# Offset convolution in four 32-column groups, the later images' first statistics beside attention 0, and the constants made behind the first norm

## The chip, the cores and the metric

The kernel runs on one core of a Trainium2 chip. The metric is the device time of one execution in microseconds (us), the median of several runs. In this text PE is TensorE (PEld its weight loads), ACT is ScalarE, DVE is VectorE, POOL is GpSimd and SP is SyncE, which here only issues transfers.

## The reference, cut to what matters

Four images x of 128 channels and 64 x 64 pixels pass four layers. Each layer starts with a group norm over 32 groups of four channels (no learned scale) and adds its result to x.

```python
x = x + layer0(_gn(x))   # attention of 4096 x 4096 scores per image, keys used as values too
x = x + layer1(_gn(x))   # involution: per-pixel 3 x 3 weights made by two 1 x 1 convolutions
x = x + layer2(_gn(x))   # 7 x 7 depthwise convolution, layer norm, MLP with gelu
x = x + layer3(_gn(x))   # deformable 3 x 3 convolution, batch norm, relu
# inside layer 3:
om = conv3x3(x, offset_w) + offset_b          # 128 -> 27 channels: 18 offsets, 9 masks
```

The change touches the 3 x 3 convolution that makes `om`, the first group norm of an image, and the preparation of constants before the first image.

## The kernel before

All engines run one hand-written program each; semaphores with counts (`wait_ge`, `then_inc`) order them. An image's 4096 pixels are handled as `NCH` = 8 chunks of 512 columns or `T` = 32 tiles of 128. There are eight PSUM banks, named in pairs `O`, `ST`, `MX`, `TR`.

**Start.** SP loads image 0 into `x_cur` and then 23 weight tensors (`w_in`). POOL clears and builds `ident`, `fold`, `gavg` and others (`pool_setup`). PE, DVE, ACT and POOL then wait for all weights and make derived constants: a bf16 high and low part of the involution weights `l1w2_s` (for this ACT first copies a bias row with three small transfers, `b2_in`, L746), the offset weights `offwb`, batch norm factors and more. Only when that is done (`dve_setup`) does each engine enter `sample(0, False)`.

**One image, `sample(n, dcn)`.** DVE waits for `x_in`, takes `bn_stats` of the eight chunks of `x_cur` (L1052) and runs `group_norm` with PE and POOL: mean over the group by a matmul with `gavg`, deviation, a second matmul, a power on POOL, the factors in `gst`. ACT then writes the normed image `xn` in four quarters (L756). From the second image on, DVE next runs `indices(n - 1)` (L1303 on), the bilinear addresses and weights for the last layer of the image before. Then comes `attention(n, dcn)`: keys and values chunk by chunk, row maxima of the first chunk (`first_maxima`, L422, reduced on DVE at L1097), and 256 steps. A step is four bf16 matmuls for scores (L464 to L467), one exponent on ACT (L779), four f32 matmuls with the values (L477) and one bf16 matmul for a maximum (L432), reduced on DVE (L1102). In images 1 to 3 the deformable convolution of the image before is run between these steps: POOL gathers patches (L1465), ACT and DVE weigh them, PE convolves. For the last image it is a tail of its own.

**End of an image, `layer3_prepare(n)`.** After the fourth norm ACT writes `xn` and its bf16 high part `xh` quarter by quarter, and DVE the low part `xl` (`low_part`, L1077, eight quarters per image over two layers). PE works on pairs of chunks: for both chunks 18 matmuls of 128 weight columns each (L668, L670). The weights hold the 27 high columns, the 27 low columns and zeros; they meet `xh` and `xl`, so rows 0 to 26 and 27 to 53 of a bank hold partial sums. Then for each chunk come four transposes of the image (L678, for the patch table) and four matmuls with `fold` (L684), which transpose and add the partial sums. ACT copies the image chunk to `xst` (L932) and evacuates the bank with the bias (L935); DVE evacuates the transposes (L1294) and the offsets (L1296). When all offsets are there (`om_rdy`), `indices` can start. SP writes the patch table in two halves of eight transfers (L352), each half as soon as the transposes of four chunks are evacuated. POOL starts gathering when `idx_rdy` and all 16 transfers of the table (`tbl_w`) are there, and in images 1 to 3 after its key work. SP loads the next image into `x_cur` when the last quarter of `xh` is written (L356).

```python
with pe.Fori(0, NCH // 2 - 1) as j:
    wait_alone(pe, s["xl_rdy"], 8 * n + 6 + j)
    two_chunks(j)
two_chunks(NCH // 2 - 1)
```

Of the kernel before, what the change touches and what calls it, by code (L numbers as in the profile page):

```python
# [13 lines left out]
BF16 = mybir.dt.bfloat16  # L14
# [49 lines left out]
def build(nc, x, wq, wk, l1w1, l1w2, l1gb, l2w1, l2w2, offw, offb, dcnw, vecs, out):  # L64
    ctx = ExitStack()
    with ctx:
# [20 lines left out]
        offwb = sb("offwb", [C, K1, 128], BF16)  # L87
# [48 lines left out]
        gst = sb("gst", [128, 8])  # L136
        ist = sb("ist", [128, NCH, 6])
# [9 lines left out]
        w2st = regk[:, 0:K1 * C].rearrange("p (k c) -> p k c", c=C)  # L147
        w2rest = regk[:, K1 * C:2 * K1 * C].rearrange("p (k c) -> p k c", c=C)
# [12 lines left out]
        slots = G[:].rearrange("p a k n -> p (a k) n")  # L161
        prod = [G[:, 0], G[:, 1], valt]
# [68 lines left out]

        def not_first(n):
            return not (isinstance(n, int) and n == 0)
# [4 lines left out]
        def wait_alone(eng, semaphore, value):  # L238
# [9 lines left out]
            "w_in pool_setup dve_setup pe_setup b2_rows b2_in bn_ve bn_pow zeroed "  # L248
# [20 lines left out]
        def _(sp):  # L269
# [39 lines left out]
            def sample(n, dcn, more):  # L309
# [4 lines left out]
                for i in range(NCH):  # L314
# [56 lines left out]
        def _(pe):  # L371
# [4 lines left out]
            pe.wait_ge(s["w_in"], 16 * WEIGHTS)  # L376
            pe.wait_ge(s["pool_setup"], 1)
            for f in range(FT):
                last = mm(P[0][:, f:f + 1], l2w1_s[:, f * 128:(f + 1) * 128], vec[:, LNB:LNB + 1],
                          start=True, stop=True)  # L380
            last.then_inc(s["pe_setup"], 1)
            nc.tensor.transpose(P[1][0:K1, 0:C], vec[:, L1B:L1B + K1], ident[:]).then_inc(s["pe_setup"], 1)
            pe.wait_ge(s["dve_setup"], 1)

            def group_norm(gi):
                pe.wait_ge(s["gn_stats"], gi + 1)
                mm(O[0][:, 0:1], gavg[:], gst[:, 0:1], start=True, stop=True).then_inc(s["gn_grp"], 1)
                pe.wait_ge(s["gn_dev"], gi + 1)
                mm(O[1][:, 0:1], gavg[:], gst[:, 3:4], start=True, stop=True).then_inc(s["gn_grp"], 1)

            def q_project(n, i):

                if i == 1:
# [5 lines left out]
            def key_chunk(n, c):  # L399
                wait_alone(pe, s["gn_xn"], 16 * n + c // 2 + 1)  # L400
                if c >= 2:
# [12 lines left out]
            def first_maxima(n, mc):  # L414

                pe.wait_ge(s["kh_rdy"], NCH * n + mc + 1)
                pe.wait_ge(s["q_rdy"], NCH * n + 1)
                for t in range(TB):
# [86 lines left out]
            def attention(n, dcn):  # L505
# [20 lines left out]
                for at in range(STEPS):  # L526
# [133 lines left out]
            def layer3_prepare(n):  # L660

                def two_chunks(j):
                    for u in range(2):
                        c = j * 2 + u
                        pe.wait_ge(s["oc_ev"], NCH * n + c + 1)
                        for k in range(K1):
                            dy, dx = k // 3 - 1, k % 3 - 1
                            mm(as_rows(ST[u][:]), offwb[:, k, :], shifted(c, dy, dx, xh),  # L668
                               start=(k == 0), stop=False)
                            last = mm(as_rows(ST[u][:]), offwb[:, k, :], shifted(c, dy, dx, xl),  # L670
                                      start=False, stop=(k == K1 - 1))
                        last.then_inc(s["oc_ps"], 1)
                    for u in range(2):
                        c = j * 2 + u
                        pe.wait_ge(s["xs_rdy"], NCH * n + c + 1)
                        pe.wait_ge(s["xt_ev"], NCH * n + c + 1)
# [859 lines left out]
```

## Time and profile before

| what | value |
|---|---|
| time, three runs | 4579.86, 4582.22 (median), 4582.42 us |
| time of the profiled execution | 4579.79 us |
| its span, first to last instruction | 4577.9 us |
| PE busy | 3952.1 us, 86% |
| DVE busy | 2862.4 us, 63% |
| ACT busy | 1779.5 us, 39% |
| POOL busy | 1454.8 us, 32% |
| mean granted clock of PE | 0.912 of full speed |

Busy time is the union of an engine's instructions. A matmul's shown duration holds its way through the pipeline, so back-to-back matmuls overlap in the record, and the distance from start to start is their price. The granted clock is given as a share of 2.4 GHz; 0.50 is 1.2 GHz.

### The profile page before, as it was taken

To read this page: it belongs to the slowest core of one execution; us is meant where nothing else is said; L and a number is where in the kernel's file an instruction comes from. 1 tells how busy PE (TensorE), PEld (TensorE's weight loads), DVE (VectorE), ACT (ScalarE), POOL (GpSimd) and SP (SyncE) were. 2 spreads that over 40 slices of the span, in tenths; PEclk is the share of its full clock that TensorE was granted. 3 is DMA by queue.
4 is the path that set the end of the run, shared out by engine and by line. 5 is a ranking of instruction groups with operands and counts; after the bars stand their busy time and mean duration, and the time that the engine had idled before them with its cause. 6 is when DMAs were issued, how large, how long until landed. Compare 5 with 4: busy or idle time off the path is not lost.

```text
span 4577.9 us, 63042 instructions
## 1 busy us (share of the span) xinstructions
PE 3952.1 (86%) x22185; PEld 2641.7 (58%) x22185; DVE 2862.4 (63%) x6449; ACT 1779.5 (39%) x3733; POOL 1454.8 (32%) x1433
## 2 busy tenths in 40 slices
PE   5999978979999968978999977988999996985555
PEld 3777733437777843435778753434787772433444
DVE  4333257757777637847777737847777746863665
ACT  2333342234555532234555543223555544122333
POOL 2000040026444323006444404005444414003775
PEclk9999989989999989988999988988999997996555
DMA  1000000045444300035445410016454420005775
GB/s 44 10 8 10 24 5 1 0 131 170 146 146 144 108 24 1 0 110 153 144 144 151 136 30 1 0 47 176 143 152 134 148 68 0 1 18 161 216 218 177
DMA packets 206392, 400.54 MB, mean 87 GB/s; under 512 B 23090, under 2 KB 121805, under 8 KB 204585
## 3 DMA queue, kind: packets, MB, share of 16 engines
q0 software_dynamic: 92160, 302.06, 22.8%
q1 hardware_dynamic: 113906, 94.92, 7.0%
q8 instruction: 162, 2.65, 0.2%
q14 instruction: 110, 0.89, 0.1%
q10 hardware_dynamic: 54, 0.01, 0.0%
HBM read 337.36 MB, written 59.53 MB: 87 GB/s over the span
## 4 chain that ended last, share of the span: by engine, by line
PE 73%; POOL 9%; issue 6%; DVE 5%; POOLq 3%; ACT 2%; DVEq 1%; DMA 1%; SPq 0%; ACTq 0%
PE bank L477 20%; PE bank L605 11%; PE bank L464 5%; PE bank L465 5%; PE bank L466 5%; PE bank L467 5%; PE bank L500 4%; PE bank L432 4%; POOL G L1465 3%; PE bank L491 2%; PE bank L631 2%; POOLq L1438 2%; PE bank L647 2%; PE bank L668 1%; PE bank L670 1%
## 5 line engine op out<-in xcount | busy, mean ns | idle before, releaser
L477 PEld LDWEIGHTS bank<-vt,pt 128*128 128x128 f32 x8192 | 1073.6, 192 | 145.6 <-issue 0.2
L477 PE MATMUL bank<-vt,pt 128*128 128x129 f32 x8192 | 1078.4, 275 | 0.0
L1102 DVE TENSOR_REDUCE mxc<-bank 128x1 f32<-128x512 f32 x896 | 617.9, 691 | 696.6 <-PE bank L432 693.8
L779 ACT ACTIVATE pt<-bank 128x512 f32<-128x512 f32 x1024 | 611.4, 597 | 905.9 <-PE bank L467 904.4
L1465 POOL DMA_INDIRECT G<-patch_table,idx x576 | 557.3, 967 | 479.9 <-DVEq L1141 248.1
L1245 DVE SCALAR_TENSOR_TENSOR G<-xn,vec,G 128x512 f32<-128x512 f32 x736 | 521.7, 748 | 47.2 <-issue 40.7
L464 PE MATMUL bank<-qh,regk 128*128 128x512 bf16 x1024 | 390.1, 381 | 3.1 <-ACT m L765 3.1
L465 PE MATMUL bank<-ql,regk 128*128 128x512 bf16 x1024 | 390.1, 381 | 0.0
L466 PE MATMUL bank<-qh,regk 128*128 128x512 bf16 x1024 | 390.1, 381 | 0.0
L467 PE MATMUL bank<-m,ones 128*128 128x512 bf16 x1024 | 389.9, 381 | 0.0
L605 PE MATMUL bank<-vt,val 128*128 (+1 forms) x1152 | 372.6, 389 | 19.5 <-DVE xl L1077 19.5
L1138 DVE SCALAR_TENSOR_TENSOR val<-G,w,val 128x128 f32<-128x128 f32 x1296 | 375.3, 346 | 7.9 <-issue 0.4
L1417 POOL TENSOR_TENSOR gst<-gst,mhalf 128x1 f32<-128x1 f32 x16 | 8.9, 558 | 1108.0 <-DVE gst L1067 1108.0
L432 PE MATMUL bank<-regk,qh 128*128 128x512 bf16 x896 | 341.8, 383 | 5.2 <-DVE mxc L1097 2.7
L1465 POOL DMA_INDIRECT regq<-patch_table,idx x256 | 245.4, 959 | 261.8 <-DVEq L1141 190.2
L1465 POOL DMA_INDIRECT x_cur<-patch_table,idx x256 | 246.9, 964 | 192.0 <-DVEq L1141 120.4
L1448 POOL TENSOR_TENSOR rs<-ve,mhalf 128x4 f32<-128x4 f32 x32 | 36.2, 1131 | 819.1 <-ACT ve L899 819.1
L500 PE MATMUL bank<-valt,dcnw_s 128*128 128x128 f32 x1728 | 240.3, 275 | 0.0
L500 PEld LDWEIGHTS bank<-valt,dcnw_s 128*128 128x128 f32 x1728 | 233.7, 191 | 11.3 <-issue 1.5
L802 ACT ACTIVATE valt<-bank 128x384 f32<-128x384 f32 x288 | 141.0, 490 | 213.9 <-PE bank L491 213.9
L605 PE MATMUL bank<-xl,val 128*128 (+1 forms) x576 | 224.0, 389 | 0.0
L605 PEld LDWEIGHTS bank<-vt,val 128*128 128x128 bf16 x1152 | 113.6, 99 | 180.0 <-issue 37.5
(231 smaller groups left out, 5913.7 us busy)
## 6 DMA issues: line engine op xcount, KB each, us to landing
patch_table<-valt SPq DMA_DIRECT2D x64, 512.0 KB, 7.1
G<-patch_table,idx POOLq DMA_INDIRECT x576, 3.7
x_cur<-in_x SPq DMA_DIRECT2D x4, 2048.0 KB, 7.9
xl<-in_x SPq DMA_DIRECT2D x32, 256.0 KB, 3.3
attn_out<-ob SPq DMA_DIRECT2D x32, 256.0 KB, 2.3
x_store<-x_cur SPq DMA_DIRECT2D x4, 2048.0 KB, 6.3
xr<-x_store SPq DMA_DIRECT2D x32, 256.0 KB, 5.4
out<-fo SPq DMA_DIRECT2D x32, 256.0 KB, 3.5
```

What stands on the lines that cost most here:

```text
L432: mm(MX[at % 2], qh[:, q0:q0 + 128], kh[:, mc * CH:(mc + 1) * CH], start=True, stop=True)\
L464: mm(bank, kh[:, tile], cols(qh, i % Q_RING), start=True, stop=False)
L465: mm(bank, kh[:, tile], cols(ql, i % Q_RING), start=False, stop=False)
L466: mm(bank, kl[:, tile], cols(qh, i % Q_RING), start=False, stop=False)
L467: mm(bank, ones2[:], m2[:, i % 2, :], start=False, stop=True).then_inc(s["st_rdy"], 1)
L477: last = mm(O[t // 2][:, (t % 2) * (C + 1):(t % 2 + 1) * (C + 1)], pt[:, at % PT_RING, t * 128:(t + 1) * 128], vt[:, st, :], start=(st == ...
L500: last = mm(TR[0][:, 384:512], dcnw_s[:, k, :], valt[:, k, piece], start=(k == 0), stop=(k == K1 - 1))
L605: last = mm(as_rows(ST[u][:]), diag(k, part), shifted(c, k // 7 - 3, k % 7 - 3, image), start=(k == 0 and image is xh and part == 0), stop ...
L779: A(pt[:, at % PT_RING, :], ST[at % ST_RING], ACT.Exp, scale=SCALE).then_inc(s["exp_done"], 1)
L1102: v.reduce_max(mxc[:, t, mc:mc + 1], MX[at % 2], AX.X).then_inc(s["mx_red"], 1)
L1245: v.scalar_tensor_tensor(acc, src, wgt, acc, ALU.mult, ALU.add)
L1465: g.indirect_dma_start(out=patches(j, k), out_offset=None, in_=table[:], in_offset=bass.IndirectOffsetOnAxis(ap=idx[:, j * K1 + k:j * K1 + ...
```

## The change

1. **Offset convolution.** `offwb` holds for each tap a 32-column block with the high part and one with the low part (27 columns used). A chunk gets 27 matmuls (per tap high x `xh`, high x `xl`, low x `xh`; low x `xl` is no longer computed). Each has 32 weight columns and writes one of four groups of 32 PSUM partitions in turn. `fold` adds four groups instead of two. PE goes chunk by chunk: the 27 matmuls of chunk c, the transposes of chunk c, the fold matmuls of chunk c - 1. Each chunk waits only for its own quarter of `xl`. The program is written out instead of looping. DVE's third and fourth quarter of `xl` come behind the first two image evacuations, and ACT copies an image chunk one ahead.
2. **Statistics.** SP loads images 1 and 2 into the idle `G` buffer behind the first table clears, and image 3 into the same place once image 1 was read. In attention 0 DVE takes their chunk statistics at every second step from steps 40, 90 and 140 on, and PE, DVE and POOL run the group norm arithmetic for each between the steps, into `gx`. Images 1 to 3 start with ACT's norm straight from `gx`; DVE goes from `layer3_prepare` directly to `indices`.
3. **Start.** The first image's statistics and norm come before the derived constants. DVE's `setup()` follows the norm; ACT's three bias row transfers follow its four norm activations. PE's first `first_maxima` and ACT's second `q_evacuate` wait for `dve_setup`. The staging area `w2st` moves from `regk` to `valt`.
4. Semaphore indices of the norms are renumbered (`norm_index`), and a few waits that the loops or the setup gave for free are written out.

```diff
-        offwb = sb("offwb", [C, K1, 128], BF16)
+        offwb = sb("offwb", [C, K1, 2, 32], BF16)
+        gx = sb("gx", [128, N, 8])
+        x_ahead = [G[:].rearrange("p a k n -> p (a k n)")[:, b * L:(b + 1) * L] for b in range(2)]
+        def ahead(q):
+            return 40 + 50 * (q - 1)
+        def image_quarter(c):
+            return min(3, (ROWS * c + ROWS) // (H // 4))
...
+            for q in range(1, 3):
+                sp.dma_start(x_ahead[(q - 1) % 2], x[q]).then_inc(s["xg_in"], 16)
...
+                    if not dcn and i == 1:
+                        sp.wait_ge(s["gn_stats"], norm_index(1, 0) + 1)
+                        sp.dma_start(x_ahead[0], x[3]).then_inc(s["xg_in"], 16)
...
+                    if not dcn:
+                        for q in range(1, N):
+                            if at == ahead(q) + 20:
+                                group_norm_first(norm_index(q, 0), TR[0], gx[:, q, :])
+                            if at == ahead(q) + 23:
+                                group_norm_second(norm_index(q, 0), TR[0], gx[:, q, :])
...
+                def offsets(c):
+                    pe.wait_ge(s["xl_rdy"], 8 * n + 4 + image_quarter(c) + 1)
+                    pe.wait_ge(s["oc_ev"], NCH * n + c + 1)
+                    for at in range(3 * K1):
+                        k, (part, image) = at // 3, ((0, xh), (0, xl), (1, xh))[at % 3]
+                        col = 32 * (at % 4)
+                        last = mm(as_rows(ST[c % 2][col:col + 32, :]), offwb[:, k, part, :],
+                                  shifted(c, k // 3 - 1, k % 3 - 1, image),
+                                  start=(at < 4), stop=(at >= 3 * K1 - 4), skip_group_check=True)
+                    last.then_inc(s["oc_ps"], 1)
...
+                for c in range(NCH):
+                    offsets(c)
+                    image_rows(c)
+                    if c:
+                        offset_rows(c - 1)
+                offset_rows(NCH - 1)
...
+            def bias_rows():
+                act.wait_ge(s["b2_rows"], 1)
+                for row in range(96, 99):
+                    act.dma_start(w2st[row:row + 1], ob[0:K1, 0:C]).then_inc(s["b2_in"], 16)
+                act.wait_ge(s["w_in"], 16 * WEIGHTS)
...
+                image_copy(0)
+                for c in range(NCH):
+                    if c + 1 < NCH:
+                        image_copy(c + 1)
+                    offset_evacuate(c)
...
+            def norm_ahead(q, r):
+                if r % 2 == 0 and 0 <= r < 2 * NCH:
+                    if r == 0:
+                        dve.wait_ge(s["xg_in"], 16 * q if q < 3 else 48)
+                    chunk_stats(r // 2, x_ahead[(q - 1) % 2])
+                if r == 18:
+                    norm_collect(gx[:, q, :])
+                if r == 21:
+                    norm_mean(norm_index(q, 0), gx[:, q, :], TR[0])
+                if r == 24:
+                    norm_variance(norm_index(q, 0), gx[:, q, :], TR[0])
+                if r == 26:
+                    norm_finish(norm_index(q, 0), gx[:, q, :])
...
+                low_part(2 * n + 1, (0, 1))
+                for c in range(NCH):
+                    image_evacuate(c)
+                    if c:
+                        offset_evacuate(c - 1)
+                    if c < 2:
+                        low_part(2 * n + 1, (c + 2,))
+                offset_evacuate(NCH - 1)
...
             def sample(n, dcn):
-                wait_alone(dve, s["x_in"], 16 * (n + 1))
-                for c in range(NCH):
-                    chunk_stats(c)
-                group_norm(4 * n)
+                if n == 0:
+                    dve.wait_ge(s["x_in"], 16)
+                    for c in range(NCH):
+                        chunk_stats(c)
+                    group_norm(norm_index(0, 0))
+                    setup()
```

## Rows read from the trace of the kernel before

**Rows 1.** Page, chain of work that ended last, by engine:
```profile
PE 73%; POOL 9%; issue 6%; DVE 5%; POOLq 3%; ACT 2%; DVEq 1%; DMA 1%; SPq 0%; ACTq 0%
```

**Rows 2.** Windows around image 0's last stage; time is busy us (count), then clock, DMA:
```profile
core 0: us, PE busy (x) PEld busy (x) DVE busy (x) ACT busy (x) POOL busy (x), PEclk, DMA share, GB/s
930.60:936.90 6.30, 0.01 (x1) 0.02 (x1) 2.46 (x2) 6.30 (x6) 1.56 (x2) 0.50 0.20 83
936.90:940.70 3.80, 3.80 (x10) 1.42 (x11) 2.11 (x2) 3.41 (x4) 0.00 (x0) 0.51 0.02 4
940.70:980.40 39.70, 39.70 (x232) 23.30 (x230) 7.72 (x16) 10.48 (x16) 0.00 (x0) 1.00 0.55 158
```

**Rows 3.** Timeline of PE, one pair of chunks, image 3: start, duration, instruction:
```profile
4133.69 0.38 PE L668 MATMUL bank<-vt,offwb 128*128 x1
...
4141.55 0.60 PE L678 MATMUL bank<-ident,xst 128*128 128x128 f32 x4
4141.98 0.97 PE L684 MATMUL bank<-fold,val 128*128 128x27 f32 x8
...
4144.08 0.38 PE L668 MATMUL bank<-vt,offwb 128*128 x1
```

**Rows 4.** Timeline, image 0's last stage and what follows it:
```profile
930.58 1.25 ACT L756 ACTIVATE xn<-x_cur,gst 128x1024 f32<-128x1024 f32 x1 [4.94 <-DVE gst L1069]
...
939.69 0.62 ACT L932 ACTIVATE xst<-xn 128x512 f32 x1
939.82 1.23 DVE L1077 TENSOR_TENSOR xl<-xn,vt 128x1024 bf16<-128x1024 f32 x1 [1.04 <-ACT vt L756]
...
980.56 0.27 DVE L1296 COPY regq<-bank 128x108 f32 x1
...
980.97 4.84 DVE L1052 BATCH_NORM_STATS2 bst<-x_cur 128x6 f32<-128x512 f32 x8
...
989.15 0.30 DVE L1307 CAST regq<-regq 128x288 f32<-128x288 int32 x1
```

**Rows 5.** Timeline of PE inside attention 0, four small transposes:
```profile
143.77 0.38 PE L443 MATMUL bank<-identb,mhl 128*2 128x128 bf16 x4
```

**Rows 6.** Timeline of the SP queue and POOL, image 3's table and the first gather:
```profile
4144.37 26.92 SPq L352 DMA_DIRECT2D patch_table<-valt  x12
...
4165.09 14.96 SPq L352 DMA_DIRECT2D patch_table<-valt  x8
...
4185.62 1.06 POOL L1465 DMA_INDIRECT G<-patch_table,idx  x1 [68.87 <-DMA patch_table<-valt]
```

**Rows 7.** Timeline of attention 0, two successive steps, DVE:
```profile
421.23 0.69 DVE L1102 TENSOR_REDUCE mxc<-bank 128x1 f32<-128x512 f32 x1 [1.28 <-PE bank L432]
...
423.20 0.69 DVE L1102 TENSOR_REDUCE mxc<-bank 128x1 f32<-128x512 f32 x1 [1.28 <-PE bank L432]
```

**Rows 8.** Timeline of the kernel's start, all engines:
```profile
13.13 0.52 POOL L1407 TENSOR_SCALAR_AFFINE_SELECT gavg<-gavg 128x128 f32<-128x128 f32 x1
...
22.08 1.87 PE L379 MATMUL bank<-vec,l2w_s 128*128 128x1 f32 x8 [22.08 <-DMA l1gb_s<-in_l1gb]
...
24.61 2.87 ACTq L746 DMA_DIRECT2D regk<-xst  x3
...
29.00 0.76 DVE L1022 CAST l1w_s<-regk 128x1152 bf16<-128x1152 f32 x1 [3.48 <-DMA regk<-xst]
...
36.65 0.21 DVE L1035 TENSOR_TENSOR dwl<-vec,dwh 128x49 f32<-128x49 f32 x1
...
38.76 4.85 DVE L1052 BATCH_NORM_STATS2 bst<-x_cur 128x6 f32<-128x512 f32 x8
...
47.64 1.28 ACT L756 ACT_TABLE_LOAD   x1 [47.64 <-DVE gst L1069]
48.94 4.67 ACT L756 ACTIVATE xn<-x_cur,gst 128x1024 f32<-128x1024 f32 x4
...
57.03 2.48 DVE L1097 TENSOR_REDUCE mxc<-bank 128x1 f32<-128x512 f32 x4 [2.07 <-PE bank L422]
```

**Rows 9.** Transfers of the first 60 us: size in KB, us from issue to landing:
```profile
x_cur<-in_x SPq DMA_DIRECT2D x1, 2048.0 KB, 8.0
```

More of the change, by code:

```diff
@@ L230, in tile_at, with norm_index @@
             return None
+        def ahead(q):
+            return 40 + 50 * (q - 1)
+        def norm_index(n, stage):
+            return N + 3 * n + stage - 1 if stage else n
+        def image_quarter(c):
+            return min(3, (ROWS * c + ROWS) // (H // 4))
         def not_first(n):
@@ L417, in first_maxima @@
                 pe.wait_ge(s["q_rdy"], NCH * n + 1)
+                if mc == 0 and n:
+                    pe.wait_ge(s["ot_ev"], NCH * n + 2)
+                elif mc == 0:
+                    pe.wait_ge(s["dve_setup"], 1)
                 for t in range(TB):
@@ new lines, in image_rows, with offset_rows @@
+                def image_rows(c):
+                    pe.wait_ge(s["xs_rdy"], NCH * n + c + 1)
+                    pe.wait_ge(s["xt_ev"], NCH * n + c + 1)
+                    for t in range(TB):
+                        last = nc.tensor.transpose(TR[c % 2][:, t * 128:(t + 1) * 128],
+                                                   xst[:, c % 2, t * 128:(t + 1) * 128], ident[:])
+                    last.then_inc(s["xt_ps"], 1)
+                def offset_rows(c):
+                    pe.wait_ge(s["oc_ev"], NCH * n + c + 1 + 2)
+                    pe.wait_ge(s["ot_ev"], NCH * n + c + 1)
+                    for t in range(TB):
+                        last = mm(MX[c % 2][:, t * NOFF:(t + 1) * NOFF], om54[:, c % 2, t * 128:(t + 1) * 128],
+                                  fold[:], start=True, stop=True)
+                    last.then_inc(s["ot_ps"], 1)
@@ L741, in _, with group_norm @@
             act.sem_inc(s["oc_ev"], 2)
-            act.wait_ge(s["w_in"], 16 * WEIGHTS)
-            act.wait_ge(s["pool_setup"], 1)
-            act.wait_ge(s["b2_rows"], 1)
-            for row in range(96, 99):
-                act.dma_start(w2st[row:row + 1], xst[0:K1, 0, 0:C]).then_inc(s["b2_in"], 16)
-            act.wait_ge(s["dve_setup"], 1)
-            def group_norm(gi, parts=False):
+            def group_norm(gi, g, parts=False):
                 act.wait_ge(s["gn_ready"], gi + 1)
@@ L828, in attention @@
                 values(NCH - 1)
+                if n == 0:
+                    act.wait_ge(s["dve_setup"], 1)
                 q_evacuate(n, 1)
@@ L1169, in attention @@
                         q_low(n, i + 2)
+                    if not dcn:
+                        for q in range(1, N):
+                            norm_ahead(q, at - ahead(q))
                     if dcn:
@@ L1398, in _ @@
                             pattern=[[-1, 128]], channel_multiplier=1)
-            for half in range(2):
-                g.affine_select(out=fold[:], in_=fold[:], compare_op=ALU.not_equal, fill=1.0, base=-half * NOFF,
+            for quarter in range(4):
+                g.affine_select(out=fold[:], in_=fold[:], compare_op=ALU.not_equal, fill=1.0, base=-quarter * 32,
                                 pattern=[[-1, NOFF]], channel_multiplier=1)
```

256 lines of the change are left out of this document (131 added, 125 removed).

## The prediction

> **What bounds the kernel.** I read the chain that ended last first: 73% of it is PE [rows 1]. So an edit counts where PE, or what PE waits for, gets shorter. The change works at three kinds of place, which I read by windows and then instruction by instruction: the last stage of each image, the seam between two images, and the first 60 us. In the last stage PE is busy without a gap for 39.7 us at the full clock, while DVE has 7.7 and ACT 10.5 us of work [rows 2]: it is bound by PE alone. At the seam the offsets are complete at 980.83, and DVE spends until 989.15 on the next image's statistics and norm before `indices` begins; the attention waits for DVE there. At the start nothing of the image is touched until 38.76 [rows 8].
>
> **Part 1, the offset convolution.** From 4133.69 to 4141.55 PE runs the 36 matmuls of a pair, 0.218 us each. Transposes and folds then take until 4144.08, 2.53 us for two chunks [rows 3]. So a chunk costs 3.93 + 1.27 = 5.2 us now, and the 1.27 stays. The new cost is X for 27 matmuls.
>
> No row of this kernel has matmuls in column groups, so X is bounded.
> - Lowest: four groups stream side by side, each matmul for 0.218 us: 27 / 4 x 0.218 = 1.47 us. Can PE be fed that fast? The four little transposes of [rows 5], each a weight load and a matmul of 128 columns, are recorded as 0.38 us together; one alone lasts 0.218, so they start 0.054 us apart. 27 x 0.054 = 1.46 us: feeding is no tighter than streaming.
> - Middle: the loads pace them. The eight fold matmuls with 128 f32 weight columns take 0.97 us together, of which one's own passage is 0.27 at most, so about 0.1 us each even with few columns [rows 3]. At 0.108, 27 give 2.9 us.
> - Highest: no overlap at all, 27 x 0.218 = 5.9 us, more than the 3.93 of today.
>
> I take 1.47 plus a drained pipeline on entering and leaving the groups. A matmul of 0.38 shown duration and 0.218 spacing leaves 0.16 us, twice, so X = 1.8. It is near the low bound because the nearest row for feeding, [rows 5], shows pairs at 0.054 with narrow weights, and these are narrow too.
>
> The Trainium skill bears on this in two ways. Its page "TensorE: Matmul & The Clock Gate", section "Measured speedup vs the span model", gives 3.07 times for four row tiles and says column tiles come within a few ns; by that X would be near 1.9, an estimate. The section "The mechanism" there says that weight loads overlap matmuls in flight only when the row group differs, which all 27 here share; what that would make of the time is rival C below.
>
> Now the stage, counted from the start of ACT's norm, 930.58 [rows 4]. Today it is 49.8 us to the end of the last fold at about 980.4. After the change:
> - ACT's order is the first limit. Its norm ends at 939.7 where the copy L932 begins, and PE's transposes of chunk 0 need that copy: 9.1 + 0.62 + 0.08 = 9.8. The convolution of chunk 0 comes before, from the first quarter of `xl`, and is hidden.
> - Transposes of chunk 0: 0.45.
> - Seven chunks, each X + 1.27: 7X + 8.9. In today's 39.7 us ACT works 10.48 us and DVE 7.72 for eight chunks [rows 2], 1.3 and 1.0 us a chunk, both below X + 1.27, so PE stays the bound. DVE's third quarter of `xl` now comes after the first image evacuation, near 943, and is needed by chunk 3, after 946.
> - The last fold, 0.82 plus 0.16 of pipeline.
> - Clock: PE stood still before and starts at 0.50 to 0.51; the first ten matmuls today take 3.8 us instead of about 2 [rows 2]. The new order leaves PE idle again after chunk 0, so I charge 2 us.
>
> Together 22.1 + 7X: 34.7 us at X = 1.8, 15.1 us less than 49.8. For images 0 to 2 that is on the path, since `indices` waits for the offsets: 45.3 us.
>
> For image 3 something else is late next, the patch table. Today SP issues the first eight transfers at 4144.37, the second eight from 4165.09 for 15.0 us, and the last lands 5.6 us after that, when POOL starts at 4185.62 [rows 6]. That is 70.4 us after the norm's start at about 4115.2, which stands 49.8 us before the end as in image 0. In the new order four chunks are evacuated at 9.8 + 0.45 + 2 + 3X + 3.0 + 0.9 = 16.1 + 3X (21.5), and eight at 21.2 + 7X (33.8). SP needs 15 us for each half, so it is SP that decides: 21.5 + 15 + 15 + 5.6 = 57.1, 13.3 us less. `indices` is done before that, 15 us after the offsets. In images 0 to 2 the same table lands at 57, while the gathers start near 66 behind POOL's key work. Part 1 gives 45.3 + 13.3 = 58.6 us.
>
> **Part 2, the statistics.** At each of three seams DVE drops the stretch from 980.97 to 989.15, 8.2 us [rows 4]; `indices` follows the offsets directly. ACT's norm needs only `gx`, the image (loaded from about 940 on; such a load took 8.0 us [rows 9]) and the last `xl`, so it starts at the same offset to `indices` as now and the overlap of both stays. 3 x 8.2 = 24.6 us.
>
> The work goes into attention 0. There a step lasts 1.97 us (421.23 to 423.20) and DVE is busy 0.69 of it [rows 7]. A chunk's statistics cost 4.84 / 8 = 0.61 us of spacing, at every second step: 1.3 us of 1.97, and the two maximum banks let PE run on meanwhile. Without this cover 24 x 0.61 = 14.5 us would come back. PE does pay: six one-column matmuls with `gavg`, two f32 passes each at the folds' pace of about 0.11, 1.3 us. The steps between the parts (18, 20, 21, 23, 24, 26) give every answer a step or more; SP's added wait at its second store is for a norm nine steps past, and nothing behind it is urgent. Part 2 gives 23.3 us.
>
> **Part 3, the start.** Everything of [rows 8], in order. The image has landed by about 9 us [rows 9]. POOL's setup ends at 13.65, now 0.4 later for two more selects, and four little DVE operations follow: statistics from 15.0. From 38.76 to 47.64 statistics and norm take 8.9 us: ready at 23.9. ACT loads its table and norms, 1.28 + 4.67: 29.9. Its three transfers (2.87 to issue, the last lands 1.5 later) end at 34.3. SP's two loads of 2 MB for images 1 and 2 start near 31.5 and share the transfer engines with them; I add 2 us: 36.3. Seven to eight wide operations on the weights, 29.00 to 36.65: dve_setup at 44.0. DVE's `q_low` over 512 columns comes next (0.8 us, as the 0.76 of such wide operations), and the first maximum at 44.8 instead of 57.03. The small operations of setup and PE's part (22.08 plus 2.2) are done while DVE would wait for the transfers. Gain 12.2 us. Bounds: 14.2 if the big loads don't hinder, and nothing, or a loss of 2, if the rows wait for both loads, 16 us.
>
> **Sum.** 58.6 + 23.3 + 12.2 = 94 us. The profiled execution took 4579.8 (span 4577.9): 4485.7. The median of the runs shown is 2.4 us above it: 4488 us.
>
> **Rivals.**
> - *A, groups side by side but paced at about 0.108 us.* X = 2.9: the stage is 42.4 us, gain 7.4 in each of three images. In image 3 the second half of the table waits for its chunks: 21.2 + 20.3 + 15 + 5.6 = 62.1, gain 8.3. Sum 30.5 + 35.5 = 66, 4516 us. For it: every fold and transpose with f32 weights runs at this pace. Against: [rows 5]. Chance 0.2.
> - *B, the groups don't overlap* (the part of the change that doesn't do what it says, and the case on the other side). X = 5.9: stage 63.4 us, 13.6 more, in three images 40.8; image 3 has 21.2 + 41.3 + 20.6 = 83.1, 12.7 more. 53.5 lost against 35.5 won: 4600 us, slower. It decides from X about 4.6 on, or 0.17 us a matmul, where the 7X take back all of parts 2 and 3. For it: 27 matmuls instead of 18 and no row that shows overlap. Chance 0.06.
> - *C, weight loads wait for the matmul before them.* Each matmul costs 0.218 plus a load's shown 0.10 (23.3 us for 230 [rows 2]), X = 8.6: stage 82.3, 32.5 more; image 3 has 102.0, 31.6 more; 129 lost, 35.5 won: about 4676 us. Against it: in the stage today 230 loads of 128 columns and 232 matmuls fit into 39.7 us of back-to-back matmuls [rows 2], with the row group the same throughout, so loads do go beside matmuls. This is what the skill's sentence on row groups above would give, and the row speaks against it. Chance 0.02.
> - *D, the start gives nothing*, because the bias rows wait behind the big loads: 12 us less gain, 4500 us. Chance 0.07.
> - *E, the statistics hinder attention 0*, all 14.5 us return: 4503 us. Against it: DVE is idle 1.28 us of each step [rows 7]. Chance 0.03.
>
> My forecast has 0.62. Cases A, D and E lie inside the range, which runs from X = 1.47 with an unhindered start (another 9 + 2 us and small change: 4470) to A with a poor start (4530). B and C are left out. This kernel can be told from no change at about 0.2%, 9 us. Faster by more 0.91, within it 0.02 (X between 4.4 and 4.8), slower 0.07.
>
> **What would show it.** In the last stage starts of 32-column matmuls 0.054 us apart, chunks 3.1 us apart, 35 us from ACT's norm to the last fold. At the seams the first L1307 cast right behind the last offset evacuation. In attention 0 still 1.97 us per step while DVE takes statistics. First maximum near 45 us. In the tail SP issues 16 table transfers without a gap. The prediction is wrong if the matmuls start 0.1 us apart or more, if the clock stays at 0.5 through the stage, or if another wait (key work, table, next image) takes over at the seam.

## The result, and the profile after

The changed kernel takes 4479.11 us (median of 4 runs, 4478.14 to 4480.61). The kernel before took 4581.04 us beside it (4 runs, 4576.1 to 4582.42). The ratio is 0.978, with a 95% interval from 0.9763 to 0.9797: 102 us less. The forecast was 4488 us, with a range from 4470 to 4530.

The page of the changed kernel, of a span of 4477.2 us: busy time of each engine, and the chain that ended last.

```profile
PE 3886.4 (87%) x22473; PEld 2605.8 (58%) x22473; DVE 2863.3 (64%) x6449; ACT 1780.8 (40%) x3733; POOL 1457.6 (33%) x1435
...
PE 73%; POOL 8%; issue 7%; DVE 4%; POOLq 3%; ACT 2%; DVEq 1%; DMA 1%; SPq 1%; ACTq 0%
```

PE's share of the chain is still 73% [rows 1], of a span that is 100.7 us shorter. PE lost 65.7 us of busy time and the other engines nearly none. So the other 35 us are not less matmul work but PE waiting less, most of it at the seams and at the start.

**The last stage.** Windows of the changed kernel, image 0: first the whole stage, from ACT's norm to the end of DVE's last offset evacuation, then its three parts. Columns as in [rows 2].

```profile
920.20:954.70 34.50, 27.58 (x312) 17.02 (x312) 12.42 (x20) 20.23 (x25) 1.58 (x2) 0.84 0.55 155
...
920.20:929.98 9.78, 3.17 (x28) 0.93 (x28) 2.46 (x2) 9.78 (x10) 1.58 (x2) 0.62 0.13 55
929.98:934.60 4.62, 4.62 (x39) 2.60 (x39) 1.95 (x3) 2.40 (x5) 0.00 (x0) 0.63 0.88 326
934.60:954.10 19.50, 19.50 (x248) 13.31 (x248) 7.74 (x15) 8.02 (x12) 0.00 (x0) 1.00 0.66 161
```

The stage takes 34.50 us; before it ran from 930.58 [rows 4] to 980.83, 50.25 us. PE is full from 929.98 on. One chunk in the middle of it, as PE's timeline of the changed kernel has it:

```profile
944.32 0.39 PE L708 MATMUL bank<-vt,offwb 128*32 128x512 bf16 x1
944.32 0.39 PE L708 MATMUL bank<-xl,offwb 128*32 128x512 bf16 x1
944.32 0.40 PE L708 MATMUL bank<-vt,offwb 128*32 128x512 bf16 x2
944.54 0.38 PE L708 MATMUL bank<-xl,offwb 128*32 128x512 bf16 x1
...
945.96 0.65 PE L717 MATMUL bank<-ident,xst 128*128 128x128 f32 x4
946.45 0.97 PE L725 MATMUL bank<-fold,val 128*128 128x27 f32 x8
947.35 0.39 PE L708 MATMUL bank<-vt,offwb 128*32 128x512 bf16 x1
```

Four matmuls, one for each column group, start at the same moment, and the next four 0.22 us later. Seven such waves bring 27 matmuls in 945.96 - 944.32 = 1.64 us. Before, 36 matmuls for two chunks came one by one, 0.218 us apart [rows 3]. A chunk now costs 3.03 us (944.32 to 947.35) where it cost 5.2.

**The seam and the last image.** Timeline of the changed kernel where image 0 ends, and for image 3 the SP queue and POOL's first gather:

```profile
954.43 0.27 DVE L1396 COPY regq<-bank 128x108 f32<-128x108 f32 x1 [0.62 <-PE bank L725]
...
954.84 0.31 DVE L1416 CAST regq<-regq 128x288 f32<-128x288 int32 x1
955.15 4.66 ACT L795 ACTIVATE xn<-x_cur,gx 128x1024 f32<-128x1024 f32 x4
...
4050.87 31.00 SPq L371 DMA_DIRECT2D patch_table<-valt  x16
...
4087.55 1.07 POOL L1572 DMA_INDIRECT G<-patch_table,idx  x1 [56.25 <-DMA patch_table<-valt]
```

`indices` follows the offsets after 0.14 us instead of 8.32 [rows 4], and ACT's norm of the next image starts from `gx` beside it. In image 3 SP issues all 16 table transfers in one run of 31.0 us; before they were two runs with a pause between [rows 6]. POOL starts 57.84 us after that image's norm (4029.71) instead of 70.45.

**Attention 0.** DVE of the changed kernel while the first norm made ahead is finished (`gx`, L1144):

```profile
207.90 0.69 DVE L1199 TENSOR_REDUCE mxc<-bank 128x1 f32<-128x512 f32 x1 [1.28 <-PE bank L466]
...
209.28 0.21 DVE L1144 TENSOR_SCALAR gx<-gx 128x1 f32<-128x1 f32 x1
209.87 0.69 DVE L1199 TENSOR_REDUCE mxc<-bank 128x1 f32<-128x512 f32 x1 [0.38 <-PE bank L466]
```

From 207.90 to 209.87 the step is still 1.97 us, as in [rows 7]. From the first to the last exponent attention 0 takes 507.98 us, where it took 506.75.

**The start.** Timeline of the changed kernel:

```profile
1.14 1.28 ACT L795 ACT_TABLE_LOAD   x1 [1.14 <-PEq L1639]
...
25.34 1.33 ACTq L801 DMA_DIRECT2D valt<-ob  x1
...
26.18 1.24 ACT L795 ACTIVATE xn<-x_cur,gst 128x1024 f32<-128x1024 f32 x1
...
29.80 0.76 DVE L1103 CAST l1w_s<-valt 128x1152 bf16<-128x1152 f32 x1 [2.33 <-DMA valt<-ob]
...
30.64 1.60 DVE L1105 TENSOR_TENSOR valt<-valt,l1w_s 128x1152 f32<-128x1152 f32 x1
...
33.20 1.14 POOL L1530 CAST regk<-xst 128x512 bf16<-128x512 f32 x1
...
33.66 0.83 SPq L298 DMA_DIRECT2D G<-in_x  x2
...
39.89 0.75 DVE L1115 CAST l1w_s<-valt 16x1152 bf16<-16x1152 f32 x1
...
41.59 2.48 DVE L1194 TENSOR_REDUCE mxc<-bank 128x1 f32<-128x512 f32 x4
...
45.43 0.61 POOL L1530 CAST regk<-xst 128x512 bf16<-128x512 f32 x1 [6.16 <-ACT xst L871]
```

The first maximum is at 41.59 instead of 57.03 [rows 8], 15.4 us earlier. ACT's bias transfers don't stand behind the norm: the first is issued at 25.34, while the second activation runs and the third (26.18) and fourth (27.31), which stand before it in the program, have yet to start. The last has landed at 29.80, before SP issues its loads for images 1 and 2 at 33.66. The first exponent is at 69.18 instead of 82.88, 13.7 us earlier.

**Where the 100.7 us of span came from**, by milestones of both traces:

| part | saved, us | forecast |
|---|---|---|
| stage, images 0 to 2 | 3 x 15.75 = 47.3 | 45.3 |
| image 3, norm to first gather | 12.6 | 13.3 |
| seams, 8.2 + 8.55 + 8.2, less 1.2 in attention 0 | 23.7 | 23.3 |
| start, at the first exponent | 13.7 | 12.2 |
| the rest: tail 2.6 (392.3 to 389.7), net of other shifts 0.8 | 3.4 | 0 |

The 0.8 is a balance of larger shifts in code that the change doesn't touch. From the last exponent of an image to its fourth norm, image 0 takes 2.1 us longer than before, and images 1 to 3 take 0.3, 2.7 and 0.7 us less. The part between the third and the fourth norm alone has the same instructions in all images of all runs and takes 232.8 to 235.8 us, with a granted clock of 0.95 in the shortest and 0.93 in the longest. The seams are counted here at the first cast of `indices`. At the first exponents of images 1 to 3 they are worth 7.8, 8.0 and 8.2 us, 24.0 instead of 24.9.

### The profile page after: what moved, and what is told of

Read it like the earlier page. It is cut to its first block, busy times and chain, and to the rows that moved or that the text cites. A ratio compares the mean times of both kernels' runs of the same rounds, so it can differ in the third digit from the quotient of the medians.

```text
span 4477.2 us, 62877 instructions
## 1 busy us (share of the span) xinstructions
PE 3886.4 (87%) x22473; PEld 2605.8 (58%) x22473; DVE 2863.3 (64%) x6449; ACT 1780.8 (40%) x3733; POOL 1457.6 (33%) x1435
## 3 DMA queue, kind: packets, MB, share of 16 engines
q0 software_dynamic: 92160, 302.06, 23.3%
## 4 chain that ended last, share of the span: by engine, by line
PE 73%; POOL 8%; issue 7%; DVE 4%; POOLq 3%; ACT 2%; DVEq 1%; DMA 1%; SPq 1%; ACTq 0%
PE bank L511 20%; PE bank L645 11%; PE bank L498 5%; PE bank L500 5%; PE bank L501 5%; PE bank L499 5%; PE bank L534 4%; PE bank L466 4%; POOL G L1572 3%; PE bank L525 2%; PE bank L671 2%; POOLq L1545 2%; PE bank L687 2%; POOL regq L1572 1%; POOL x_cur L1572 1%
## 5 line engine op out<-in xcount | busy, mean ns | idle before, releaser
L1555 POOL TENSOR_TENSOR rs<-ve,mhalf 128x4 f32<-128x4 f32 x32 | 36.3, 1134 | 821.0 <-ACT ve L948 821.0
L534 PE MATMUL bank<-valt,dcnw_s 128*128 128x128 f32 x1728 | 240.3, 275 | 0.0
L771 PE MATMUL bank<-valt,dcnw_s 128*128 128x128 f32 x576 | 130.2, 420 | 93.3 <-ACT valt L1032 93.3
```

Source lines behind the costliest of these rows:

```text
L534: last = mm(TR[0][:, 384:512], dcnw_s[:, k, :], valt[:, k, piece], start=(k == 0), stop=(k == K1 - 1))
```

## The experiments

Each run undoes or changes one thing of the changed kernel (e9 two, e5 none). Some were run on chips where the attentions of images 1 to 3, in which POOL gathers patches, take longer with every kernel, the one before included (last section). There whole times compare only with runs on the same chip (e1 to e4 on one, e9 to e12 on another), and stretches without gathers decide, since these agree with the other chips. This table has them in us. "Stage" is ACT's fourth norm to the last offset evacuation, "seam" from there to the first cast of `indices`, "gather" image 3's norm to its first gather.

| kernel | first max | first exp | attention 0 | stage | seam | gather |
|---|---|---|---|---|---|---|
| before | 57.03 | 82.88 | 506.8 | 50.25 | 8.32 | 70.45 |
| changed | 41.59 | 69.18 | 508.0 | 34.50 | 0.14 | 57.84 |
| e5_control | 41.56 | 69.07 | 507.6 | 34.50 | 0.14 | 57.79 |
| e1_same_group_runs | 41.60 | 68.30 | 508.2 | 45.38 | 0.14 | 65.24 |
| e6_two_groups | 40.83 | 67.68 | 508.2 | 43.48 | 0.14 | 63.3 |
| e2_wide_by_chunk | 40.75 | 68.27 | 508.4 | 47.87 | 0.14 | 67.18 |
| e12_wide_by_chunk | 40.86 | 68.38 | 508.4 | 47.87 | 0.14 | 67.26 |
| e3_stats_at_seam | 41.62 | 69.14 | 507.0 | 34.50 | 8.31 | 57.87 |
| e10_stats_at_seam | 41.56 | 69.08 | 506.7 | 34.50 | 8.31 | 57.78 |
| e4_setup_first | 55.96 | 81.81 | 508.2 | 34.50 | 0.14 | 57.79 |
| e11_setup_first | 55.37 | 81.22 | 507.9 | 34.50 | 0.14 | 57.98 |
| e7_copies_between_quarters | 41.67 | 69.18 | 507.7 | 30.16 | 0.14 | 53.14 |
| e8_lag_five | 41.94 | 66.83 | 508.4 | 34.50 | 0.14 | 57.97 |
| e9_both | 41.95 | 66.85 | 508.2 | 30.2 | 0.14 | 53.3 |

### The groups: same matmuls, another order of groups

```diff
-                        col = 32 * (at % 4)
+                        col = 32 * (at // 7)
...
-                                  start=(at < 4), stop=(at >= 3 * K1 - 4), skip_group_check=True)
+                                  start=(at % 7 == 0), stop=(at % 7 == 6 or at == 3 * K1 - 1),
+                                  skip_group_check=True)
```

> The changed kernel with one edit: the 27 matmuls of a chunk still write four groups of 32 columns, but in runs (7, 7, 7, 6) of the same group instead of in turn. Theory (neighbours in different groups stream together, in 7 waves of 0.218 us): without different neighbours only the three borders between runs can overlap, a chunk's matmuls take about 25 x 0.218 = 5.4 us instead of 1.64, the last stage grows from 34.5 to about 61 us, and the kernel takes about 4479 + 4 x 26 = 4583 us. Rival (32-column matmuls are cheap by themselves, whatever their order, or PE looks far enough ahead in its queue to pair them): no change, 4479 us.

Measured: stage 45.38 us, 10.9 more than the changed kernel. Whole time 5098.85 us against 5154.85 of the kernel before on that chip, ratio 0.9885 (0.9863 to 0.9907). PE's timeline of this run, one chunk:

```profile
950.53 0.39 PE L708 MATMUL bank<-vt,offwb 128*32 128x512 bf16 x1
950.75 0.38 PE L708 MATMUL bank<-xl,offwb 128*32 128x512 bf16 x1
...
951.19 0.60 PE L708 MATMUL bank<-xl,offwb 128*32 128x512 bf16 x2
...
953.64 0.38 PE L708 MATMUL bank<-vt,offwb 128*32 128x512 bf16 x1
953.95 0.66 PE L718 MATMUL bank<-ident,xst 128*128 128x128 f32 x4
```

Neighbours in one group start 0.22 us apart, no closer than in one queue; only matmuls of different groups start together. But the chunk's 27 matmuls take 953.95 - 950.53 = 3.42 us, not the 5.4 that was expected. Each next group's first matmul starts with the fourth of the seven before it, so two groups run side by side for most of the time. That is not the order of the program: the line at 951.19 joins two `xl` matmuls that start one after the other, while in the program every `xl` stands between two of `xh` (`vt` in the trace). The first of the two starts together with the run's fourth, so it belongs to the next group: it is the eighth matmul of the chunk, and it starts before the fifth, the second of the two. So in this run PE let a matmul of another group pass three that stood before it. A chunk takes 4.82 us, 1.8 more than in the changed kernel. That the gain comes from interleaving is shown; that runs of one group lose nearly all of it is refuted.

### Two groups instead of four

```diff
-                        col = 32 * (at % 4)
+                        col = 32 * (at % 2)
...
-                                  start=(at < 4), stop=(at >= 3 * K1 - 4), skip_group_check=True)
+                                  start=(at < 2), stop=(at >= 3 * K1 - 2), skip_group_check=True)
...
-            for quarter in range(4):
+            for quarter in range(2):
```

> The changed kernel with the 27 matmuls alternating between two groups of 32 columns only. Theory (waves as wide as there are groups, 0.218 us each): 14 waves instead of 7, a chunk's matmuls 3.15 instead of 1.64 us, the last stage 34.5 + 7 x 1.5 = 45 us. Rival (four groups are not what sets the pace, loads or issue are): under 40 us.

Measured: 4505.72 us in one run, against 4479.45 for the control; stage 43.48. PE's timeline of this run:

```profile
937.20 0.39 PE L708 MATMUL bank<-vt,offwb 128*32 128x512 bf16 x1
937.21 0.39 PE L708 MATMUL bank<-xl,offwb 128*32 128x512 bf16 x1
937.43 0.39 PE L708 MATMUL bank<-vt,offwb 128*32 128x512 bf16 x2
...
940.36 0.66 PE L717 MATMUL bank<-ident,xst 128*128 128x128 f32 x4
```

Now two start together and 14 waves follow, 0.22 us apart: 3.16 us to the transposes in place of 1.64. The price goes by waves, and feeding is no limit: a pace of 0.108 us a matmul (rival A) would give nearly the same for two groups, 2.9, but it would give it for four as well, and four took 1.64.

### Wide matmuls in the new order

This kernel keeps the change's order by chunks, but with 18 matmuls of 128 weight columns per chunk, as the kernel before had. A matmul takes two neighbouring blocks of 64 columns, and `fold` reads only the first 54 rows of the result, the 27 high and the 27 low ones.

```diff
-        offwb = sb("offwb", [C, K1, 2, 32], BF16)
+        offwb = sb("offwb", [C, K1 + 1, 64], BF16)
...
-                    for at in range(3 * K1):
...
+                    for at in range(2 * K1):
+                        k, image = at // 2, (xh, xl)[at % 2]
+                        last = mm(as_rows(ST[c % 2][:]), offwb[:, k:k + 2, :].rearrange("p k o -> p (k o)"),
+                                  shifted(c, k // 3 - 1, k % 3 - 1, image),
+                                  start=(at == 0), stop=(at == 2 * K1 - 1))
```

> The changed kernel with the 18 matmuls of 128 weight columns per chunk back, in the new order of chunks (27 matmuls gone, rows 54 to 127 of the bank hold sums that fold leaves out). Theory (the groups give the gain of the last stage, the order of chunks next to nothing): chunks 3.93 + 1.4 = 5.3 us apart, the stage near 49.5 us as before, time about 4479 + 3 x 15.5 + 13 = 4539 us. Rival (chunk by chunk, with waits per quarter, gives much of it): the stage clearly under 45 us, time under 4520 us.

Measured: stage 47.87 us; 5103.32 us, ratio 0.989 (0.9867 to 0.9913). PE's timeline of this run, one chunk:

```profile
939.69 0.38 PE L707 MATMUL bank<-vt,offwb 128*128 128x512 bf16 x1
...
943.61 0.60 PE L716 MATMUL bank<-ident,xst 128*128 128x128 f32 x4
...
944.86 0.38 PE L707 MATMUL bank<-vt,offwb 128*128 128x512 bf16 x1
```

So of the 15.75 us that a stage lost, the order by chunks gives 2.4 and the column groups 13.4. A chunk costs 5.2 us as before. What the order gives lies at the start: the first matmul stands 3.7 us behind ACT's norm (922.76 - 919.06) instead of 6.3. It was run again on another chip:

> The kernel with the 18 wide matmuls back in the new order of chunks. Theory: the stage takes 47.9 instead of 34.5 us in images 0 to 2 as in the run before, and 10 to 13 us are lost before the first gather of image 3: 4479.5 + 40 + 11 = 4531 us.

Measured: 5197.03 us, ratio 0.9913 (0.9881 to 0.9945), the same stage of 47.87.

### The statistics back at the seam

```diff
-            return N + 3 * n + stage - 1 if stage else n
+            return 4 * n + stage
...
-            for q in range(1, 3):
-                sp.dma_start(x_ahead[(q - 1) % 2], x[q]).then_inc(s["xg_in"], 16)
...
-                            norm_ahead(q, at - ahead(q))
...
+                    wait_alone(dve, s["x_in"], 16 * (n + 1))
+                    for c in range(NCH):
+                        chunk_stats(c)
+                    group_norm(norm_index(n, 0))
```

> The changed kernel with only the statistics put back: DVE takes them at the start of images 1 to 3, nothing of them is done beside attention 0, the two images are not loaded ahead. Theory (8.2 us at each of three seams, paid for by 1.2 us of PE in attention 0): 4479 + 24.7 - 1.2 = 4502.5 us, `indices` starts 8.2 us later after the offsets, attention 0 is 1.2 us shorter from first exponent to the next norm. Rival (the work beside attention 0 costs more than it shows, or the start of `indices` was not what the attention waits for): less than 15 us lost.

Measured: 5090.07 us, ratio 0.9862 (0.9832 to 0.9891). DVE of this run at the seam:

```profile
951.65 0.27 DVE L1384 COPY regq<-bank 128x108 f32<-128x108 f32 x1 [0.62 <-PE bank L714]
952.06 4.84 DVE L1113 BATCH_NORM_STATS2 bst<-x_cur 128x6 f32<-128x512 f32 x8
...
960.23 0.30 DVE L1404 CAST regq<-regq 128x288 f32<-128x288 int32 x1
```

The seam is 8.31 us again, and attention 0 is 1.0 us shorter. A seam saves 8.17 us at the first cast, and the three together cost 1 us in attention 0. It was run once more on another chip:

> The kernel with only the statistics put back to the seams, now on a chip that is hoped to gather at the speed of the first. Theory: 8.2 us at each of three seams less 1 us in attention 0, 4479.5 + 23.7 = 4503 us. Rival: less than 15 us lost.

Measured: 5163.17 us, ratio 0.9855 (0.9823 to 0.9888); seam 8.31, attention 0 shorter by 1.2. The milestones carry this reading, since whole times on these chips vary by more.

### The setup back in front of the first norm

```diff
                 if n == 0:
+                    setup()
                     dve.wait_ge(s["x_in"], 16)
...
                     group_norm(norm_index(0, 0))
-                    setup()
...
-                    group_norm(0, gst)
                     bias_rows()
+                    act.wait_ge(s["dve_setup"], 1)
+                    group_norm(0, gst)
```

> The changed kernel with only the start put back: constants first, then the first image's statistics and norm. Theory (the start gives 13.7 us at the first exponent): 4493 us, first exponent near 83 us as before. Rival (what is won at the first maximum, 15.4 us, is real, and the later loss is from elsewhere): 4494.5 us and a first exponent later than 84 us.

Measured: 5075.98 us, ratio 0.984 (0.9817 to 0.9862); first maximum 55.96, first exponent 81.81. The order is worth 14.4 us at the first maximum and 12.6 at the first exponent. DVE of this run, the same operations as in the start above, now with no work on POOL beside them:

```profile
29.92 0.76 DVE L1104 CAST l1w_s<-valt 128x1152 bf16<-128x1152 f32 x1 [2.25 <-DMA valt<-ob]
30.75 1.36 DVE L1106 TENSOR_TENSOR valt<-valt,l1w_s 128x1152 f32<-128x1152 f32 x1
...
36.81 0.75 DVE L1116 CAST l1w_s<-valt 16x1152 bf16<-16x1152 f32 x1
```

The eight take 7.6 us here (29.92 to 37.56) and 10.8 in the changed kernel (29.80 to 40.64). It was run again:

> The kernel with only the order at the start put back. Theory: 12.7 to 13.7 us lost, as the first exponents of the runs so far show, 4493 us.

Measured: 5160.36 us, ratio 0.9854 (0.9822 to 0.9887); first exponent at 81.22.

### Control, copies between the norm's quarters, and a longer lag

These ran on a chip like the first, so that whole times decide. First the changed kernel again:

> The changed kernel itself, so that the kernels of this call have it on their own chip. The theory expects the same gain in microseconds as on the first chip, about 100 us over the kernel before; if gathers are slow on this chip the whole is longer for both and the ratio a little nearer to 1.

Measured: 4479.45 us (4476.92 to 4480.23), before 4576.58; ratio 0.9785 (0.977 to 0.98).

The stage spends its first 9.78 us behind ACT: eight norm activations in a row, then the copy `xst` that PE's transposes need. PE is done with chunk 0's convolution 2.91 us before that and stands idle. The next kernel puts the copies between the quarters.

```diff
+                norm_quarter(gst, 0, True)
                 image_copy(0)
-                for c in range(NCH):
-                    if c + 1 < NCH:
-                        image_copy(c + 1)
+                norm_quarter(gst, 1, True)
+                image_copy(1)
+                norm_quarter(gst, 2, True)
+                offset_evacuate(0)
+                image_copy(2)
+                norm_quarter(gst, 3, True)
+                for c in range(1, NCH):
                     offset_evacuate(c)
+                    if c + 2 < NCH:
+                        image_copy(c + 2)
```

> The changed kernel with ACT's order in the last stage changed: the copies of chunks 0, 1 and 2 and the first evacuation stand between the quarters of the norm instead of behind all four. Theory (PE idles from the end of chunk 0's matmuls until the first copy, 3.8 us, and then runs chunk 1 at half clock, which costs another 1.6 us): PE's chunk 1 starts about 2.7 us earlier and warm, 3 to 4.5 us less per stage, 12 to 18 us in all. Rival (the quarters, 0.6 us later each for every copy, then hold the later chunks): under 1.5 us per stage.

Measured: 4458.8 us (4456.56 to 4459.32), ratio 0.9739 (0.9726 to 0.9752): 20.65 us less than the control. PE where chunk 0 ends and chunk 1 begins, first in the changed kernel, then in this one:

```profile
929.98 0.65 PE L717 MATMUL bank<-ident,xst 128*128 128x128 f32 x4 [2.91 <-ACT xst L980]
930.56 0.39 PE L708 MATMUL bank<-vt,offwb 128*32 128x512 bf16 x1
...
930.79 0.46 PE L708 MATMUL bank<-xl,offwb 128*32 128x512 bf16 x1
...
931.05 0.63 PE L708 MATMUL bank<-vt,offwb 128*32 128x512 bf16 x1
...
931.48 0.63 PE L708 MATMUL bank<-xl,offwb 128*32 128x512 bf16 x1
```
```profile
926.44 0.89 PE L717 MATMUL bank<-ident,xst 128*128 128x128 f32 x4
927.26 0.39 PE L708 MATMUL bank<-vt,offwb 128*32 128x512 bf16 x1
...
928.90 0.66 PE L717 MATMUL bank<-ident,xst 128*128 128x128 f32 x4
```

In the changed kernel PE stands still for 2.91 us. It then runs two waves 0.23 us apart, and the rest of chunk 1 at twice the distance (931.05, 931.48), which is the clock of 1.2 GHz: granted clock 0.63 in the window 929.98 to 934.60. The chunk needs 2.76 us for its 27 matmuls (930.56 to 933.32) where a full-clock one needs 1.64. In this kernel PE goes on without that gap, and its chunk 1 takes 1.64 us (927.26 to 928.90). The stage is 30.16 us, in the later images 29.89: 4.35 and 4.6 less. With 4.65 in image 3 (57.79 to 53.14) that is 18.2 of the 20.65; part of the rest lies behind each seam, where the first exponent follows 0.6 to 0.9 us sooner.

The other edit lets the score steps of image 0 start later in the key work (`lag = 5` as in the other images), so that POOL makes all keys without a break.

```diff
-                lag = 5 if dcn else 2
+                lag = 5
...
-                    if at == TB * (NCH - lag) + (8 if dcn else 4):
+                    if at == TB * (NCH - lag) + 8:
```

> The changed kernel with one edit in image 0: the first maxima come five key chunks later (as in the other images) instead of two, so PE, ACT and POOL go on with keys while DVE still makes constants. Theory (of 15.4 us won at the first maximum 1.7 are lost until the first exponent because the key work stopped at chunk 2): the first exponent comes 2 to 4 us earlier, 66 us instead of 69.2. Rival (POOL's key work slows DVE's constants as it does from 30 to 39 us already, and what is won is lost in front of the first maximum): no change within 1 us.

Measured: 4476.55 us (4476.09 to 4478.81), ratio 0.9781 (0.9768 to 0.9794): 2.9 less than the control by the medians, but the ranges overlap, so the whole time leaves it open. The milestone does not: the first exponent is at 66.83, 2.2 us earlier. In the changed kernel DVE takes the chunks' maxima in groups of four, 2.7 us apart, while POOL's key cast comes once in each such group; with the longer lag POOL's casts follow every 1.87 us (43.82, 45.69, 47.56) and the maxima run on.

### Both edits together

> The changed kernel with both improvements: ACT's copies between the quarters of the norm in the last stage (20.7 us less by itself) and five instead of two key chunks ahead of the first maxima in image 0 (2.9 us less by itself). They lie in different stages, so the theory is that they add: 4479.5 - 23.6 = 4456 us, 2.65% below the kernel before. Rival (the second only moves the wait): 4459 us.

Measured: 5118.36 us (5099.91 to 5130.71) against 5243.84 for the kernel before on that chip, ratio 0.9768 (0.974 to 0.9796). On the same chip e10, e11 and e12 had 5163.17, 5160.36 and 5197.03. The stage (30.2) and the first exponent (66.85) show both edits whole. The fastest time on a chip like the first is 4458.8 us for the copies alone. Both together were not run there, nor was the changed kernel beside them here. With the 2.2 us of the earlier first exponent, 4457 us is an estimate.

## Why the prediction was right, step by step

**X, the 27 matmuls.** Forecast 1.8, measured 1.64 us. Seven waves of 0.218 are 1.53 us, which leaves 0.11 for leaving the groups. The price of entering them lies outside X: the rest of a chunk, which the forecast took over as 1.27, is 1.39 us (945.96 to 947.35), where e2 has 1.25 for the same transposes and folds behind 128-column matmuls. Both changes together cost about 0.25 us and not 0.32. So X was put 0.16 too high and the rest 0.12 too low, and the chunk came out right, 3.07 forecast and 3.03 measured, because the two nearly cancel. The picture behind the low bound was half right. Matmuls do stream four abreast, but they are not fed 0.054 us apart: they start together, so the sign named for it would not have been found. Rivals A (2.9), B (5.9) and C (8.6) fell with the same rows. Against no overlap, 27 x 0.218 = 5.9, it is 3.6 times as fast, more than the 3.07 times for four row tiles of the Trainium skill's page "TensorE: Matmul & The Clock Gate", section "Measured speedup vs the span model". The section "The mechanism" there ties the overlap of weight loads to a change of row group. All 27 share theirs, and the loads still went beside the matmuls: 312 of each in 27.58 us of busy PE.

One sum behind the rivals was wrong: B was to decide from X about 4.6 on, and the change to be indistinguishable for X between 4.4 and 4.8. By the forecast's own terms a chunk's X counts 28 times (seven chunks in each of four images), the loss of part 1 is 28X - 111.7, and it reaches the 35.5 us of parts 2 and 3 at X = 5.3. The forecast time doesn't hang on it.

**The stage.** Forecast 34.7, measured 34.50. The first 9.8 us behind ACT were right (9.78). The clock charge of 2 us was 1.6: from chunk 1's first matmul to chunk 2's it takes 4.65 us (930.56 to 935.21), where the others take 3.03. The reason given for it, that PE would stand idle after chunk 0, is what the trace shows, and e7 is the test: without the idle time the charge is gone. Counted to the last fold, as the forecast did, the stage took 34.2. The 0.5 us of difference are 0.4 of clock and 0.3 of seven chunks, less 0.1 for chunk 0's transposes. In the table above the stages save 2.0 us more than forecast.

**Image 3.** 57.1 forecast, 57.84 measured. The chain was the one named: fourth evacuation, SP's 16 transfers in one run of 31.0 us (30 forecast), and 5.7 us from there to POOL's first gather. That SP decides and not the convolution is seen again in e7, where the gather comes 53.14 us after the norm: SP starts 16.5 us behind the norm instead of 21.2, and its run is again 30.9 us. With the slower convolution of e1 and e2 it is 65.2 and 67.2. In e2 SP takes 35.5 us for the 16, since the second half waits for its chunks.

**The seams.** 24.6 forecast, 24.9 measured at the first casts and 24.0 at the first exponents, with 1.3 and 1.2 us for attention 0; e3 and e10 gave each back alone.

**The start.** This is the step that was mis-sized: 12.2 forecast, 15.4 measured at the first maximum and 13.7 at the first exponent. The forecast put ACT's three bias transfers behind its table load and four norm activations (end at 34.3) and added 2 us for the big loads. In the trace the table load stands at 1.14, off the path, and the transfers are issued between the activations from 25.34 on. They had landed at 29.8, 6.5 us before the 36.3 that was assumed, and ahead of the big loads. Half of that was lost again to a thing the forecast didn't have: the wide DVE operations, priced at their durations in the kernel before, ran 3.2 us longer beside POOL's key work. Rival D was based on the same wrong place of the transfers. Another 1.7 us went between the first maximum and the first exponent, 27.6 us now and 25.85 before. The reason is the key work, which used to be far ahead by then: e8 starts the exponents 2.2 us sooner by giving the keys a lead.

**Rival E** had no support: the step is 1.97 us with statistics in it.

**Expectations behind the prediction that were wrong in size.** e1 was to take 5.4 us a chunk and a stage of about 61; PE let the next group in early, and it took 3.42 and 45.4. e2's stage was to be near 49.5 and was 47.9, since the order by chunks is worth 2.4 us. e7 was to save 12 to 18 us and saved 20.65.

What stays open is the 2.6 us by which the tail is shorter, and the shifts of up to 2.7 us between an image's last exponent and its fourth norm. The control's tail took 391.1 us with the same code, so 1.4 us of it varies from run to run. The forecast had all of this at nothing, and that it adds up to only 3.4 us is no merit of it.

## What to carry to other kernels

When a matmul needs 32 weight columns or fewer, write the accumulating matmuls to four column groups in turn, even if it takes half as many again: 27 went through in 1.64 us where 18 took 3.93. Put neighbouring instructions in different groups: runs of seven in one group took 3.42 us. Then look at what feeds the first one: here 9.8 of the stage's 34.5 us were ACT's order, and copies put between norm quarters gave 20.65 us more, part of it because PE no longer stood still and fell to the lower clock. Statistics of a tensor that is known beforehand cost next to nothing in a stretch where their engine idles two thirds of the time, and about 8 us where the next stage waits for them.

## What the runs showed of the hardware

- Four matmuls with 32 weight columns in different column groups start within 0.02 us of each other; two groups give pairs, and a run of seven in one group gives 0.22 us each, with the next group's first matmul let in ahead of the last three of the run (e1).
- To go from 128-column matmuls to 32-column ones and back cost about 0.25 us a chunk: 3.03 us less seven waves (1.53) and e2's 1.25.
- ACT's queue issued transfers while its activations were still running (the first at 25.34, where the last activation before it in the program starts at 27.31). Here they didn't wait for what stands before them to end.
- DVE and POOL slowed each other at the start. A subtract of 128 x 1152 took 1.60 us beside POOL's key work and 1.36 alone, a cast of 2 x 1152 took 1.56 and 0.76; POOL's cast of 128 x 512 took 1.14 us there and 0.61 later. With POOL's key work lasting longer (e8) the last of the eight DVE casts took 1.07 us instead of 0.75.
- Gathers ran slower on some chips with everything else equal. A window of 400 us in image 1's gathers, the changed kernel on the first chip and then e1 on another:

```profile
1100.00:1500.00 400.00, 400.00 (x2793) 318.75 (x2792) 291.08 (x816) 209.88 (x477) 191.08 (x198) 1.00 0.50 145
```
```profile
1100.00:1500.00 400.00, 342.96 (x2166) 266.20 (x2167) 227.16 (x639) 162.14 (x373) 146.66 (x153) 0.92 0.39 112
```

PE has no gap in the first and 57 us of gaps in the second, and the transfers move 112 GB/s instead of 145. From first to last exponent such an attention takes 603 us on the one kind of chip and 772 to 804 on the other, and the tail 390 against 457 to 475. Stretches without gathers agree, image 0's stage to 0.1 us. Why these chips gather more slowly was not looked into. The whole time there is longer and varies more, so ratios found there don't carry over.
